# A Fourier block on one core: TensorE's loop unrolled five times, ScalarE's row transfer moved, half of x added on TensorE for three row groups

## The chip, the core and the metric

The kernel runs on one core of a Trainium2 chip. The core has five engines that run at the same time, each with an instruction queue of its own, and wait for each other by semaphores: TensorE (matrix products, PE in the profile, its weight loads PEld), VectorE (DVE), ScalarE (ACT), GpSimd (POOL) and SyncE (SP), which here only issues DMAs. All but GpSimd and SyncE read PSUM, the memory of 8 banks into which TensorE writes. The metric is the device time of one execution in microseconds (us); lower is better.

## The reference

x has the shape (4, 128, 128, 768). For each image and channel: a two-dimensional real Fourier transform, a small two-layer network with complex weights on each block of 96 channels at every frequency, the transform back, and x added.

```python
xf = jnp.fft.rfft2(x, axes=(1, 2), norm='ortho')            # 128 x 65 frequencies
xr, xi = real(xf), imag(xf)      # reshaped to 8 blocks of 96 channels
o1r = relu(xr @ w1[0] - xi @ w1[1] + b1[0])
o1i = relu(xi @ w1[0] + xr @ w1[1] + b1[1])
o2r = o1r @ w2[0] - o1i @ w2[1] + b2[0]
o2i = o1i @ w2[0] + o1r @ w2[1] + b2[1]
o2r, o2i = softshrink(o2r, 0.01), softshrink(o2i, 0.01)
out = jnp.fft.irfft2(o2r + 1j * o2i, s=(128, 128), axes=(1, 2), norm='ortho') + x
```

## The kernel before

The work is cut into 32 units q, one for each image and block of 96 channels. A unit's x stands in SBUF as 128 partitions (one image axis) by 128 rows h by 96 channels; two buffers `xs[0]` and `xs[1]` take turns. Every engine runs its own program: a part ahead, a hardware loop over `STEPS - 1` = 15 steps with two units each (p = 0 and 1), and the last step written out. At the end of a step each engine has a branch back to the loop's first instruction.

Stages of a unit, as TensorE goes through them:

- `keep_warm` (L635): four products whose result nobody reads; `transform_row0` (L499): row 0 of the next unit, which has a way of its own (`row0`, copied by ScalarE in `copy_row0`, L752, and moved by two DMAs that ScalarE issues in `move_row0`, L756 and L757, into row 127 of `ydg` and of `yedge`).
- `inverse_lines` (L515): 26 line groups of 4 or fewer channels, back along h. ScalarE and VectorE copy each result from PSUM to `ydg` and pack the input of the one five groups later into `rings`.
- rows (`first_rows`, `rows`, L646 to L649): 13 row groups g of five rows, back along the other axis. A group has an odd part v and an even part u, in two PSUM banks; the 8 banks hold four groups, so group g waits until VectorE is done with group g - 4 (`uv_ready`). `add_halves` (L972, L979) on VectorE adds half of the folded x to u (into `ucopy`) and to v (into the x buffer) in one instruction of 2 x 480 columns. GpSimd then forms sum and difference of the two (L1051, L1053), which are the output rows, and SyncE stores them in seven batches, followed by the loads of the unit after next.
- `forward_lines` (L493, L494) of the next unit: 26 line groups again. `packer_a` and `mover` say which of ScalarE and VectorE packs the input of a group (L733, L870) and which copies its result (L743, L882). The first five packs stand at the end of ScalarE's previous unit. The line banks are those of the rows, so the first groups wait for the last `uv_ready`.
- mixing (L536 to L629): ten frequency groups, transform along h, first layer in split precision, relu on ScalarE, second layer, shrink on VectorE. The areas that it uses (`zbig`, `zhi`, `hbig`, `biased` and others) lie over `ucopy`. ScalarE's first copy into `zbig` (L768) and VectorE's first shrink therefore wait for the last store batch's rows (`wait_batch`).

TensorE runs the unit boundary as: rows of q, forward lines and mixing of q + 1, then keep-warm of q + 1; its branch stands between the mixing and the keep-warm products. ScalarE's branch stands behind `move_row0`, between rows and forward lines. VectorE's stands between its first mixing operations, GpSimd's behind the last sums.

At the start SyncE issues the transform table, the 16 loads of unit 0 (four pieces of 16 + 16 rows, each in two halves of 64 partitions), the rest of the table, weights, and the 16 loads of unit 1. VectorE folds x (L864, L866: sums and differences of mirrored rows) as the pieces land.

## Time and profile before

| | |
|---|---|
| three runs, us | 4975.51, 4975.89, 4977.45 |
| median, us | 4975.89 |
| profiled execution, us | 4975.77 |
| its span on the core, us | 4973.7 |
| TensorE busy | 4779.5 us, 96% of the span |
| VectorE busy | 4070.3 us, 82% |
| ScalarE busy | 2514.4 us, 51% |
| GpSimd busy | 1028.1 us, 21% |
| DMA over the span | 421.33 MB, mean 85 GB/s |
| mean granted TensorE clock | 0.989 of full speed |

Busy time counts what an engine executes. Matrix products overlap, so a busy TensorE is not one at its best pace. Idle time that "issue" ends is time in which the engine waited for nothing that the profile shows; branches and semaphore instructions are not shown. One fp32 product leaves two records. The profile's times start with the span.

### The profile page before, as it was taken

What the parts mean: (1) busy time and instruction counts of PE and PEld (TensorE: products, weight loads), DVE (VectorE), ACT (ScalarE), POOL (GpSimd) and SP (SyncE); (2) the same over time, 40 slices, a digit from 0 to 9 for tenths busy, and PEclk for the clock granted to TensorE, in tenths of its full rate; (3) what the DMA queues carried; (4) which work ended last, traced back from release to release, by engine and by line L of the source; (5) the groups of instructions that cost most, each with busy time, mean ns of one, the idle gap of its engine ahead of it and who ended that gap; (6) DMA issues with size and microseconds to landing.
All of it is one profiled execution on the core that took longest, in us unless ns stands there. A gap on an engine that the chain in (4) does not pass through costs nothing.

```text
span 4973.7 us, 120408 instructions
## 1 busy us (share of the span) xinstructions
PE 4779.5 (96%) x44930; PEld 3997.2 (80%) x44930; DVE 4070.3 (82%) x6763; ACT 2514.4 (51%) x4290; POOL 1028.1 (21%) x836
## 2 busy tenths in 40 slices
PE   6999999999999999999999999999999999999997
PEld 5888888888888887888878788788888888788886
DVE  5888888888888888888888888788887888888876
ACT  4554455545555445555445554455544555445553
POOL 0220222211222112222022220122211222102222
PEclk9999999999999999999999999999999999999999
DMA  6422544324443234442344423444224453234522
GB/s 110 102 60 51 107 104 104 77 45 95 103 103 87 43 86 103 103 99 44 74 103 103 108 50 62 101 103 108 63 61 88 103 108 78 59 76 103 107 53 51
DMA packets 1079029, 421.33 MB, mean 85 GB/s; under 512 B 1076128, under 2 KB 1076256, under 8 KB 1078432
## 3 DMA queue, kind: packets, MB, share of 16 engines
q1 hardware_dynamic: 1073696, 411.61, 39.1%
q8 instruction: 395, 6.47, 0.6%
q10 hardware_dynamic: 4736, 1.60, 0.1%
q14 instruction: 202, 1.65, 0.1%
HBM read 210.19 MB, written 201.33 MB: 83 GB/s over the span
## 4 chain that ended last, share of the span: by engine, by line
PE 85%; DVE 6%; issue 5%; ACT 3%; POOL 1%; SPq 0%; ACTq 0%; DMA 0%; DVEq 0%; POOLq 0%
PE ps L515 14%; PE ps L611 13%; PE ps L493 10%; PE ps L536 10%; PE ps L620 6%; PE ps L548 5%; PE ps L594 5%; PE ps L582 4%; PE ps L646 3%; PE ps L561 3%; PE ps L569 2%; PE ps L562 2%; ACT rings L733 2%; DVE ydg L954 1%; DVE biased L929 1%
## 5 line engine op out<-in xcount | busy, mean ns | idle before, releaser
L1051 POOL TENSOR_TENSOR whole<-whole 128x480 f32<-128x480 f32 (+1 forms) x416 | 499.4, 1200 | 3904.0 <-DVE whole L979 3904.0
L743 ACT COPY ydg<-ps 128x512 f32<-128x512 f32 (+4 forms) x1024 | 588.3, 578 | 571.4 <-PE ps L494 352.9
L611 PE MATMUL ps<-wts,hbig 128*128 128x192 f32 x4160 | 735.1, 328 | 4.3
L493 PEld LDWEIGHTS ps<-tab,rings 128*64 128x64 f32 x6144 | 675.3, 138 | 78.8 <-ACT rings L733 42.7
L493 PE MATMUL ps<-tab,rings 128*64 128x128 f32 x6144 | 701.2, 275 | 35.1 <-ACT rings L733 34.2
L515 PE MATMUL ps<-tab,rings 128*128 128x128 f32 x6144 | 712.1, 280 | 15.9 <-DVE rings L949 15.9
L515 PEld LDWEIGHTS ps<-tab,rings 128*128 128x128 f32 x6144 | 708.0, 196 | 18.8 <-DVE rings L949 17.9
L494 PE MATMUL ps<-tab,rings 128*63 128x128 f32 x6144 | 701.4, 275 | 0.0
L611 PEld LDWEIGHTS ps<-wts,hbig 128*128 128x128 f32 x4160 | 672.1, 190 | 20.6 <-ACT hbig L791 13.7
L494 PEld LDWEIGHTS ps<-tab,rings 128*63 128x63 f32 x6144 | 675.0, 137 | 0.0
L929 DVE TENSOR_TENSOR biased<-ps,wts 128x768 f32<-128x768 f32 (+1 forms) x544 | 498.9, 917 | 194.0 <-PE ps L620 189.4
L733 ACT COPY rings<-whole 128x508 f32<-128x508 f32 (+1 forms) x608 | 617.5, 1086 | 0.1
L536 PEld LDWEIGHTS ps<-tab,ydg 128*128 128x128 f32 x4032 | 501.3, 191 | 105.5 <-issue 91.6
L536 PE MATMUL ps<-tab,ydg 128*128 128x128 f32 x4032 | 562.3, 282 | 22.0 <-DVE ydg L882 22.0
L768 ACT COPY zbig<-ps 128x512 f32<-128x512 f32 (+1 forms) x544 | 307.6, 569 | 523.2 <-PE ps L536 474.8
L1053 POOL TENSOR_TENSOR whole<-whole 128x480 f32<-128x480 f32 (+1 forms) x416 | 544.6, 1309 | 34.7
L791 ACT ACTIVATE hbig<-ps,wts 128x1024 f32<-128x1024 f32 (+1 forms) x320 | 305.5, 955 | 426.4 <-PE ps L594 426.4
L882 DVE COPY ydg<-ps 127x512 f32<-127x512 f32 (+5 forms) x640 | 388.3, 631 | 157.6 <-PE ps L494 125.8
L954 DVE TENSOR_TENSOR ydg<-biased,clamped 128x768 f32<-128x768 f32 (+1 forms) x512 | 477.7, 933 | 16.7
L907 DVE TENSOR_TENSOR zlo<-zbig,zhi 128x1024 fp32r<-128x1024 f32 (+1 forms) x320 | 326.2, 1019 | 195.4 <-ACT zhi L775 195.4
L875 DVE TENSOR_TENSOR rings<-ydg 128x248 f32<-128x248 f32 (+3 forms) x672 | 379.8, 565 | 114.9 <-PE ps L515 112.2
L782 ACT CAST zsmall_hi<-ps 128x512 fp32r<-128x512 f32 (+1 forms) x320 | 163.2, 510 | 586.2 <-PE ps L548 586.2
(82 smaller groups left out, 8893.8 us busy)
## 6 DMA issues: line engine op xcount, KB each, us to landing
out<-whole SPq DMA_DIRECT2D x704, 240.0 KB, 4.2
whole<-in_x SPq DMA_DIRECT2D x384, 384.0 KB, 6.5
whole<-in_x SPq DMA_DIRECT2D x64, 408.0 KB, 7.8
whole<-in_x SPq DMA_DIRECT2D x64, 360.0 KB, 6.7
out<-whole SPq DMA_DIRECT2D x64, 216.0 KB, 3.5
wts<-in_mix SPq DMA_DIRECT2D x16, 513.0 KB, 4.9
out<-whole SPq DMA_DIRECT2D x64, 120.0 KB, 3.2
out<-whole SPq DMA_DIRECT2D x64, 96.0 KB, 2.9
```

Source lines behind the costliest of these rows:

```text
L493: pe.matmul(o[0:HALF], slot[:, 0:HALF], mat("fwd_w"), start=True, stop=True)
L494: mm = pe.matmul(o[HALF:127], slot[:, HALF:127], mat("fwd_w_odd"), start=True, stop=True)
L515: mm = pe.matmul(ps[:, line_bank(1, g), j * 128:(j + 1) * 128], ring[g % RING][:, j, :], mat("inv_h"), start=True, stop=True)
L536: mm = pe.matmul(ps[:, z_bank(u, h), k * H:(k + 1) * H], t[:, s:s + 2, :].rearrange("p k c -> p (k c)")[:, 0:BIG], mat("fwd_h"), start=Tru ...
L611: mm = pe.matmul(o, hbig[:, k * H:(k + 1) * H], mix_part("w2_big"), start=first, stop=False, skip_group_check=True)
L733: act.copy(*line_pack_moves(p, g)).then_inc(line_packed_act, 1)
L743: act.copy(*line_moves(stage, g)).then_inc(line_act, 1)
L882: dve.tensor_copy(*line_moves(stage, g)).then_inc(line_dve, 1)
L929: dve.tensor_tensor(parts(v), d, b2, ALU.add).then_inc(bias_done, 1)
L954: dve.tensor_tensor(dst, parts(v)[:, :, first:ne, :], parts(c)[:, :, first:ne, :], ALU.subtract).then_inc(shrunk, 1)
L1051: pool.tensor_tensor(xs[p][:, a:b, :], u, xm, ALU.add).then_inc(y_plus, 1)
L1053: pool.tensor_tensor(xm, u, xm, ALU.subtract).then_inc(batch_ready[batch_of(g)], batch_part(g))
```

## The change

Six things are changed.

1. **TensorE's loop** has five steps in its body (`UNROLL`) and runs three rounds in place of 15.
2. **ScalarE**: `move_row0` no longer stands at the end of a unit but inside the forward lines, ahead of line group 6 (`MOVE_ROW0_AT`), and waits for the previous unit's last `uv_ready`. In its place stand three copies (below), and behind them the loop's branch.
3. **Half of x on TensorE**, for row groups 4, 6 and 8 (`ADDED`): the even part gets a third pair of products, half the identity times the folded x rows. ScalarE copies u out of PSUM into `ucopy` and counts `u_copied`; VectorE's operation treats v alone (480 columns, not 2 x 480) and waits for v alone. GpSimd, and TensorE where it takes the bank again (group + 4), wait for `u_copied`.
4. **Waits for the store batches**: ScalarE's first `zbig` copy has none now; its first `zsmall` rounding waits for the batch of group 1, VectorE's first small remainder for that of group 4, ScalarE's first relu for that of group 7. VectorE's first shrink keeps its wait for the last.
5. **Start**: SyncE loads the lower 64 partitions of unit 0 and ScalarE issues the loads of the upper 64, at once.
6. **End**: in the last unit VectorE forms the sums and differences of row groups 6 to 12, after its last `add_halves`; GpSimd does groups 0 to 5.

The first place is the end of ScalarE's loop body and its beginning: end of a unit, branch, forward lines (`rings<-whole` are packs, `ydg<-ps` copies of line results). Before:

```order
L841 ISA
L756 DMA ydg<-row 1x128x96 [waits row0_copied,u_done,v_done]
L757 DMA yedge<-row 1x2x96
L851 REGISTER_ALU
L851 COMPARE_AND_BRANCH
L743 COPY ydg<-ps 127x128x4 [waits line_done]
L733 COPY rings<-whole 128x4x127 [waits line_done]
L743 COPY ydg<-ps 127x128x4 [waits line_done]
L733 COPY rings<-whole 128x4x127 [waits line_done]
L743 COPY ydg<-ps 127x128x4 [waits line_done] x2
```

and changed:

```order
L870 COPY whole<-ps 128x480 [waits u_done]
L881 REGISTER_ALU
L881 COMPARE_AND_BRANCH
L767 COPY ydg<-ps 127x128x4 [waits line_done]
L755 COPY rings<-whole 128x4x127 [waits line_done]
L767 COPY ydg<-ps 127x128x4 [waits line_done]
L755 COPY rings<-whole 128x4x127 [waits line_done]
L767 COPY ydg<-ps 127x128x4 [waits line_done] x2
L755 COPY rings<-whole 128x4x127 [waits line_done] x2
L781 DMA ydg<-row 1x128x96 [waits row0_copied,uv_ready]
L782 DMA yedge<-row 1x2x96
L767 COPY ydg<-ps 127x128x4 [waits line_done]
```

The two DMAs went behind the copies of line groups 0 to 3 and the packs of 5, 6, 8 and 9; the last of the copies of u stands ahead of the branch.

The second place is TensorE in the rows, groups 4 and 5 (`ps<-ydg,tab` are the products of v and u). Before:

```order
L654 ISA
L646 MATMUL ps<-ydg,tab 64x480 [waits uv_ready]
L647 MATMUL ps<-ydg,tab 64x480
L648 MATMUL ps<-ydg,tab 64x480
L649 MATMUL ps<-ydg,tab 64x480
L654 REGISTER_ALU
L646 MATMUL ps<-ydg,tab 64x480 [waits uv_ready]
```

and changed:

```order
L674 ISA
L661 MATMUL ps<-ydg,tab 64x480 [waits uv_ready]
L662 MATMUL ps<-ydg,tab 64x480
L664 MATMUL ps<-ydg,tab 64x480
L665 MATMUL ps<-ydg,tab 64x480
L668 MATMUL ps<-whole,tab 64x480
L669 MATMUL ps<-whole,tab 64x480
L674 REGISTER_ALU
L661 MATMUL ps<-ydg,tab 64x480 [waits uv_ready]
```

The pair `ps<-whole,tab`, which reads the x buffer, was added between group 4's u and group 5's v.

The third place is ScalarE's program from its first instruction, in the changed kernel; before, it began with the table load.

```order
L875 DMA whole<-in_x 64x16x96
L875 DMA whole<-in_x 64x15x96
L875 DMA whole<-in_x 64x16x96 x4
L875 DMA whole<-in_x 64x17x96
L875 DMA whole<-in_x 64x16x96
L755 ACT_TABLE_LOAD [waits pairs_folded]
L755 COPY rings<-whole 128x4x127 [waits cleared]
L755 COPY rings<-whole 128x4x127 x4
L776 COPY row<-ps 128x96 [waits row0_done]
```

Eight of the 16 loads of unit 0 moved here from SyncE, and the row's transfers that followed the last line are gone from this place.

The diff, cut to its core (left out: two semaphores declared, a scratch tile `scrap` in place of `clamped` for the initial settings):

```diff
 NF = HC // HG
+POOL_LAST = 6
+ADDED = (4, 6, 8)
 AREA = 60 * H + 28 * CB
...
 LOAD_AFTER = {2: 0, 4: 1, 6: 2}
+MOVE_ROW0_AT = 6
+UNROLL = 5
 for _name, _n in (("fwd_w", W), ("fwd_w_odd", W), ("fwd_h", H), ("inv_h", H), ("inv_w_even", HALF), ("inv_w_odd", HALF),
-                  ("merge_even", H), ("merge_odd", H)):
+                  ("merge_even", H), ("merge_odd", H), ("half", HALF)):
     COLS[_name] = (_at, _at + _n)
...
     return np.concatenate([fwd_w / 128, fwd_w_odd / 128, fwd_h, inv_h, inv_even / 128, inv_odd / 128,
-                           merge_even, merge_odd], 1).astype(np.float32)
+                           merge_even, merge_odd, np.concatenate([np.eye(64), np.eye(64)]) / 2], 1).astype(np.float32)
...
+        def piece_rows(i):
+            a, e = i * LOAD_ROWS, (i + 1) * LOAD_ROWS
+            return (a, e + (e == HALF)), (H + 1 - e, H + 1 - max(a, 1))
         def odd_rows(g):
             return max(HG * g, 1), min(HG * g + HG, H // 2)
+        def wait_added(engine, q, g):
+            if g in ADDED:
+                engine.wait_ge(u_copied, len(ADDED) * q + ADDED.index(g) + 1)
...
-                def load_piece(n, b, p, i):
+                def load_piece(n, b, p, i, parts=(0, 1)):
                     src = x[bass.ds(b, 1), :, :, bass.ds(n * CB, CB)].rearrange("o h (m t) c -> (o t) m h c", t=2)
-                    a, e = i * LOAD_ROWS, (i + 1) * LOAD_ROWS
-                    for lo, hi in ((a, e + (e == HALF)), (H + 1 - e, H + 1 - max(a, 1))):
-                        for t in range(2):
+                    for lo, hi in piece_rows(i):
+                        for t in parts:
                             sp.dma_start(xs[p][t * HALF:(t + 1) * HALF, lo:hi, :],
...
-                load_x(0, 0, 0)
+                for i in range(PIECES):
+                    load_piece(0, 0, 0, i, (0,))
                 sp.dma_start(tab[:, FWD:TABLE], table[:, FWD:TABLE]).then_inc(table_loaded, 16)
...
-                def quarters(g, cols):
+                def quarters(p, g, cols):
...
                     mv = pe.matmul(v[top], odd[low], yv[low], start=True, stop=True)
-                    pe.matmul(u[top], even[top], yu[top], start=True, stop=True)
-                    mu = pe.matmul(u[low], even[low], yu[low], start=True, stop=True)
+                    alone = g not in ADDED
+                    pe.matmul(u[top], even[top], yu[top], start=True, stop=alone)
+                    mu = pe.matmul(u[low], even[low], yu[low], start=True, stop=alone)
+                    if not alone:
+                        half, xp = mat("half"), xs[p][:, a:b, cols]
+                        pe.matmul(u[top], half[top], xp[top], start=False, stop=True)
+                        mu = pe.matmul(u[low], half[low], xp[low], start=False, stop=True)
                     return mv, mu
-                def rows(q, g):
+                def rows(q, p, g):
                     if g >= 4:
                         pe.wait_ge(uv_ready, NF * q + NF + g - 3)
+                        wait_added(pe, q, g - 4)
                         pe.sem_inc(row_banks_free, 1)
-                    mv, mu = quarters(g, slice(0, CB))
+                    mv, mu = quarters(p, g, slice(0, CB))
                     mv.then_inc(v_done, 1)
-                def first_rows(q):
+                def first_rows(q, p):
                     pe.sem_inc(row_banks_free, 1)
-                    quarters(0, slice(0, c))
+                    quarters(p, 0, slice(0, c))
                     lines_moved(q, 1)
                     pe.sem_inc(row_banks_free, 1)
-                    mv, mu = quarters(0, slice(c, CB))
+                    mv, mu = quarters(p, 0, slice(c, CB))
                     mv.then_inc(v_done, 1)
...
                         inverse_lines(q)
-                        first_rows(q)
+                        first_rows(q, p)
                         for g in range(1, NF):
-                            rows(q, g)
+                            rows(q, p, g)
                         if not (last and p == PAIRS - 1):
...
                 to_inverse(0, 0, 0)
-                with pe.Fori(0, STEPS - 1) as t:
-                    step(t, False)
+                with pe.Fori(0, (STEPS - 1) // UNROLL) as rounds:
+                    for i in range(UNROLL):
+                        step(rounds * UNROLL + i, False)
                 step(STEPS - 1, True)
...
                     for g in range(NG):
+                        if stage == 0 and g == MOVE_ROW0_AT:
+                            move_row0(q)
                         if mover(stage, g) == "act":
...
                 def move_row0(q):
+                    act.wait_ge(uv_ready, NF * q + NF)
                     act.wait_ge(row0_copied, q + 1)
                 def copy_big(q, u, h):
-                    if u == 0 and h == 0:
-                        wait_batch(act, q - 1, NF - 1)
                     act.wait_ge(zbig_done, NP * q + part_at(u, h))
...
                 def round_small(q, u):
+                    if u == 0:
+                        wait_batch(act, q - 1, 1)
                     act.wait_ge(zsmall_done, NU * q + u + 1)
...
                     act.wait_ge(big_mixed, NU * q + u + 1)
-                    if u:
+                    if u == 0:
+                        wait_batch(act, q - 1, 7)
+                    else:
                         act.wait_ge(hbig_read, NU * q + u)
...
                                 pack_lines(q + 1, 1 - p, g)
-                            act.wait_ge(v_done, NF * q + NF)
-                            act.wait_ge(u_done, NF * q + NF)
-                            move_row0(q + 1)
+                        for g in ADDED:
+                            act.wait_ge(u_done, NF * q + g + 1)
+                            act.copy(ucopy[g].rearrange("p h c -> p (h c)"),
+                                     ps[:, row_bank(g), 0:HG * CB]).then_inc(u_copied, 1)
+                first = x[0:1, :, :, 0:CB].rearrange("o h (m t) c -> (o t) m h c", t=2)
+                for i in range(PIECES):
+                    for lo, hi in piece_rows(i):
+                        act.dma_start(xs[0][HALF:W, lo:hi, :], first[1, :, lo:hi, :]).then_inc(x_loaded[0][i], 16)
                 act.wait_ge(cleared, 1)
                 copy_row0(0)
-                move_row0(0)
                 with act.Fori(0, STEPS - 1) as t:
...
                     dve.wait_ge(zsmall_hi_ready, NU * q + u + 1)
+                    if u == 0:
+                        wait_batch(dve, q - 1, 4)
                     dve.tensor_tensor(zsmall_lo[u % 2][0:r, 0:n], ps[0:r, z_bank(u, "small"), 0:n],
...
                     dve.wait_ge(v_done, NF * q + g + 1)
+                    if g in ADDED:
+                        xm, v = xs[p][:, H - b + 1:H - a + 1, :], ps[:, row_bank(g) + 1, 0:HG * CB]
+                        dve.scalar_tensor_tensor(xm, xm, 0.5, v.rearrange("p (h c) -> p h c", c=CB),
+                                                 ALU.mult, ALU.add).then_inc(uv_ready, 1)
+                        return
                     dve.wait_ge(u_done, NF * q + g + 1)
...
+                def last_sums(q, p, g):
+                    a, b = odd_rows(g)
+                    u, xm = ucopy[g][:, 0:b - a, :], mirror(xs[p], a, b)
+                    dve.wait_ge(uv_ready, NF * q + NF + g + 1)
+                    wait_added(dve, q, g)
+                    dve.tensor_tensor(xs[p][:, a:b, :], u, xm, ALU.add).then_inc(last_plus, 1)
+                    dve.wait_ge(last_plus, g - POOL_LAST + 1)
+                    dve.tensor_tensor(xm, u, xm, ALU.subtract).then_inc(batch_ready[batch_of(g)], batch_part(g))
                 def wait_loaded(p, times, i):
...
                             add_halves(q, p, g)
+                        if not fold_next:
+                            for g in range(POOL_LAST, NF):
+                                last_sums(q, p, g)
                         if fold_next:
                 dve.memset(yedge[:], 0.0).then_inc(cleared, 1)
-                dve.memset(clamped[0:1, 0:1], 0.0).then_inc(uv_ready, NF)
-                dve.memset(clamped[0:1, 1:2], 0.0).then_inc(y_plus, NF)
+                dve.memset(scrap[0:1, 0:1], 0.0).then_inc(uv_ready, NF)
+                dve.memset(scrap[0:1, 1:2], 0.0).then_inc(y_plus, NF)
                 for i, ready in enumerate(batch_ready):
-                    dve.memset(clamped[0:1, 2 + i:3 + i], 0.0).then_inc(ready, 2)
+                    dve.memset(scrap[0:1, 2 + i:3 + i], 0.0).then_inc(ready, 2)
                 dve.wait_ge(uv_ready, NF)
...
             def _(pool):
-                def step(t):
+                def step(t, last):
                     for p in range(PAIRS):
                         q = t * PAIRS + p
-                        for g in range(NF):
+                        for g in range(POOL_LAST if last and p == PAIRS - 1 else NF):
                             a, b = odd_rows(g)
                             pool.wait_ge(uv_ready, NF * q + NF + g + 1)
+                            wait_added(pool, q, g)
                             pool.tensor_tensor(xs[p][:, a:b, :], u, xm, ALU.add).then_inc(y_plus, 1)
-                with pool.Fori(0, STEPS) as t:
-                    step(t)
+                with pool.Fori(0, STEPS - 1) as t:
+                    step(t, False)
+                step(STEPS - 1, True)
```

## Rows read from the trace of the kernel before

**Rows 1.** The page, part 4: the chain that ended last, by engine.

```profile
PE 85%; DVE 6%; issue 5%; ACT 3%; POOL 1%; SPq 0%; ACTq 0%; DMA 0%; DVEq 0%; POOLq 0%
```

**Rows 2.** Timeline of TensorE, keep-warm products: start us, us, engine, line, operation, idle before.

```profile
1845.46 1.16 PE L635 MATMUL ps<-tab 128*128 128x128 f32 x8
...
2001.47 2.07 PE L635 MATMUL ps<-tab 128*128 128x128 f32 x8 [2.75 <-issue]
...
2152.81 1.16 PE L635 MATMUL ps<-tab 128*128 128x128 f32 x8
...
4610.31 1.16 PE L635 MATMUL ps<-tab 128*128 128x128 f32 x8
...
4760.24 1.16 PE L635 MATMUL ps<-tab 128*128 128x128 f32 x8
```

**Rows 3.** Waits of TensorE: who waited, for what, us in total, times, longest.

```profile
PE ps L635 <- issue: 39.0, 14, 3.1
```

**Rows 4.** Timeline of ScalarE: start of the run, a step with its branch, one without.

```profile
47.50 0.59 ACT L743 COPY ydg<-ps 127x512 f32<-127x512 f32 x1 [1.98 <-PE ps L494]
...
1886.68 0.59 ACT L743 COPY ydg<-ps 127x512 f32<-127x512 f32 x1 [12.00 <-PE ps L494]
...
4646.31 0.53 ACTq L756 DMA_DIRECT2D ydg<-row  x1
4646.87 0.83 ACTq L757 DMA_DIRECT2D yedge<-row  x1
4647.88 0.59 ACT L743 COPY ydg<-ps 127x512 f32<-127x512 f32 x1 [8.36 <-PE ps L494]
```

**Rows 5.** Timeline of TensorE: first forward product (L493), first mixing products (L536).

```profile
1906.73 1.71 PE L536 MATMUL ps<-tab,ydg 128*128 128x128 f32 x13 [0.67 <-DVE ydg L882]
...
4646.23 0.32 PE L493 MATMUL ps<-tab,rings 128*64 128x128 f32 x1
...
4668.29 1.82 PE L536 MATMUL ps<-tab,ydg 128*128 128x128 f32 x14 [0.69 <-DVE ydg L882]
```

**Rows 6.** Timeline of ScalarE: the five packs at the end of a unit.

```profile
4634.38 5.14 ACT L733 COPY rings<-whole 128x508 f32<-128x508 f32 x5
```

**Rows 7.** Windows: us, busy time of five engines, granted clock, DMA share, GB/s.

```profile
2001.00:2003.00 2.00, 1.53 (x7) 1.53 (x8) 0.00 (x0) 0.00 (x0) 0.00 (x0) 0.50 0.03 8
```

**Rows 8.** Timeline of TensorE: first row products, two groups further on, then forward lines.

```profile
2026.73 0.51 PE L646 MATMUL ps<-ydg,tab 64*64 64x352 f32 x1
...
4634.22 0.51 PE L646 MATMUL ps<-ydg,tab 64*64 64x352 f32 x1
...
4638.21 0.56 PE L646 MATMUL ps<-ydg,tab 64*64 64x480 f32 x1
...
4639.01 0.56 PE L646 MATMUL ps<-ydg,tab 64*64 64x480 f32 x1
...
4647.04 0.27 PE L493 MATMUL ps<-tab,rings 128*64 128x128 f32 x1
...
4647.29 0.32 PE L493 MATMUL ps<-tab,rings 128*64 128x128 f32 x1
```

**Rows 9.** Timeline of VectorE in the rows: twelve operations in one row.

```profile
4635.57 12.65 DVE L979 SCALAR_TENSOR_TENSOR whole<-whole,ps 128x768 f32<-128x768 f32 x12
```

**Rows 10.** Timeline of VectorE at the start: folds behind a landed piece.

```profile
25.69 1.16 DVE L864 TENSOR_TENSOR whole<-whole 128x960 f32<-128x960 f32 x1 [2.56 <-DMA whole<-in_x]
...
33.13 1.16 DVE L864 TENSOR_TENSOR whole<-whole 128x960 f32<-128x960 f32 x1 [5.09 <-DMA whole<-in_x]
```

**Rows 11.** Windows: loads alone; large rows; stores and loads together.

```profile
5.00:10.00 5.00, 0.00 (x0) 0.00 (x0) 0.00 (x0) 0.00 (x0) 0.00 (x0) 1.00 1.30 224
...
33.00:34.00 1.00, 0.00 (x0) 0.00 (x0) 0.87 (x1) 0.00 (x0) 0.00 (x0) 1.00 1.02 378
...
210.00:220.00 10.00, 9.28 (x152) 8.92 (x149) 8.08 (x14) 5.59 (x10) 8.71 (x8) 1.00 1.16 253
```

**Rows 12.** Timeline of SyncE's queue: the stores of the last unit.

```profile
4940.73 30.84 SPq L461 DMA_DIRECT2D out<-whole  x28
```

5 lines of the change are left out of this document (4 added, 1 removed).

## The prediction, written before the changed kernel ran

> **What bounds the kernel now.** I read the chain of waits first. 85% of it is TensorE and 6% VectorE, so what counts is each time that TensorE stands still or runs slowly [rows 1]. One set of 32 (image, channel block) units follows another, and TensorE's four keep-warm products mark the start of each. Near the end of the run one unit takes 4760.24 - 4610.31 = 149.93 us. In the middle a unit with odd number takes 2001.47 - 1845.46 = 156.01, and the even one behind it 2152.81 - 2001.47 = 151.34 [rows 2]. A loop step is an odd and an even unit; the units at the end run where no engine's loop branch is taken any more. So a step costs 307.35 - 2 * 149.93 = 7.5 us more with branches than without. TensorE waited 14 times, 39.0 us in all, for nothing that the profile shows, right before the keep-warm products [rows 3]: 14 of its 15 branches are taken, the last falls through. That is where to look, since the same instructions stand in both kinds of unit.
>
> **ScalarE's branch.** In the odd unit without a taken branch, ScalarE issues the two transfers of row 0 and copies the first group of forward lines at 4647.88, 8.36 us after its last copy. With the branch it does so at 1886.68, after 12.00 us: the stall is 3.64 us [rows 4]. From the keep-warm products to TensorE's first product of the mixing it is then 1906.73 - 1845.46 = 61.27 us against 4668.29 - 4610.31 = 57.98 [rows 5]. The branch costs 3.29 us, in 14 units: 46 us. The change puts the three copies of u where the transfers stood and the branch behind them; the transfers go into the forward lines, before group 6. Is the stall covered there? ScalarE's five packs end at 4634.38 + 5.14 = 4639.5 [rows 6]. The last copied group is 8. By its own pace (below) TensorE ends it 9 * 0.80 + 3 * 0.40 = 8.4 us after the start of the rows at 4634.22, near 4642.6, and the copy ends at 4643.2. With the stall ScalarE is back at 4646.8. TensorE's first forward group, which it has to copy, starts near 4634.22 + 11.6 = 4645.8 and ends 0.9 us later, at 4646.7. So the stall is hidden, narrowly, and I take all **46 us**. Each us that the stall is longer would come straight on 14 units.
>
> **TensorE's branch.** What is left of the 7.5 us: the odd unit has 156.01 - 149.93 - 3.29 = 2.79 us of idleness beyond what the waiting for VectorE would cost anyway, and the even one is 151.34 - 149.93 = 1.41 us longer. The second is the clock: after the idle time the granted clock is 0.50 (1.2 of 2.4 GHz) [rows 7], and the way from keep-warm to the rows takes 2026.73 - 2001.47 = 25.26 us against 4634.22 - 4610.31 = 23.91 [rows 2, 8]. A taken branch costs 4.20 us. The loop of 15 steps becomes 3 rounds of 5: two taken branches instead of 14, 12 * 4.20 = **50 us**. What is late next there is VectorE's last shrink; that wait is in the 149.93 already. The body is five times as long, but the code behind the loop, never run before, is entered by the fall-through without a stall (no idle time before the products at 4760.24 [rows 2]).
>
> **Rows: half of x on TensorE.** Without a wait, TensorE does a row group in 4639.01 - 4638.21 = 0.80 us, two pairs of products of 0.40 each [rows 8]. VectorE does twelve groups in 12.65 us, 1.06 each [rows 9], and there are banks for four groups only, so TensorE ends up at VectorE's pace: 4646.23 - 4634.22 = 12.01 us for 13 groups [rows 5, 8]. The change gives TensorE a third pair in three groups: 13 * 0.80 + 3 * 0.40 = 11.6. VectorE loses half of three operations, 3 * 0.5 us, and is at no point the later one. TensorE becomes the bound and 0.41 us go. The small gap between the first two forward groups (4647.29 - 4647.04, against 0.11 between neighbours [rows 8]) waits for the tenth-last sums and goes with VectorE's gain, 0.14. ScalarE's copies (0.59 us for 512 columns [rows 4]) lie in its idle time; group 8 needs the copy of group 4, done near 4640.1, at 4641.4. 31 units * 0.55 = **17 us**. The pair is not in the trace of before. If it overlapped badly and cost 0.80, the sum would be 12.8 us for the rows, and 20 us lost; if it cost nothing VectorE's pace would bound and some 40 us would be gained. I take 0.40: the same 64x64 shape on the same columns.
>
> **Row 0 inside the lines.** The two issues take 0.53 + 0.83 us [rows 4], at a place where ScalarE has little slack: forward packs run one behind the other and TensorE needs each about 0.7 us after it is done. If the issues stop the engine for their full 1.4 us, TensorE waits about 0.65 in each of 31 units, 20 us; if they pass while earlier copies still run, 0. I take **-3 us**, nearer to nothing, because the five packs stand in one row without a gap [rows 6], so copies are handed over ahead of time. The Trainium skill ("Advanced Engine Details and Errata", Sequencer Loop) says that engine instructions wait in a queue while the sequencer works on others; by that alone this term would be 0.
>
> **Start.** VectorE's folds start when a piece of x has landed, 33.13 - 25.69 = 7.4 us apart [rows 10]; the fold of the last piece leads to TensorE's start. The loads run at 224 GB/s; where stores and loads are mixed it is 253, and with large rows of all partitions once 378 [rows 11]. The change issues the upper half from ScalarE at the same time. Bounds: nothing, or four pieces at 378 (4 * 3.0 = 12 us). At 253, 4 * 7.4 * (1 - 224/253) = 3.4. ScalarE's first line copy no longer stands behind row 0's transfers (idle for 1.98 us before 47.50 [rows 4]): up to 1.7, I take 1.5. Together **5 us**. On the first part the Trainium skill speaks with two voices. "DMA: Bandwidth & Descriptors" (Rules for kernel authors) advises against two transfers to disjoint partition halves, since they share the same 16 engines: 0, and 4862 in all. "SBUF — State Buffer" (Door 1) says that 64 partitions reach only half of the ports, which would make the two halves together up to twice as fast. The 224 GB/s fit the second, but no row has both halves in flight.
>
> **End.** VectorE takes over the last 7 of GpSimd's groups. The stores are 28 issues in 30.84 us [rows 12]; 6.3 MB at 253 GB/s are 24.9. The first three batches keep GpSimd's pace, and VectorE's additions may hold GpSimd up. **1 us**, bounds 0 and 3. The waits for single store batches instead of the last one free ScalarE's first copy of the mixing; TensorE has the other products of that group to do first, so it is worth nothing now, but it lets the earlier arrival through.
>
> **Sum.** 46 + 50 + 17 - 3 + 5 + 1 = 116 us, rounded 117 with the fractions (46.1, 50.4). The profiled execution took 4975.77 (span 4973.7), the median of three runs is 4975.89: no difference here. 4975.8 - 117 = **4859 us**.
>
> **Rivals.**
> 1. The transfers of row 0 do stop ScalarE, or its branch stall isn't covered: up to +20 or so, 4870 to 4885. For it: the slack of 0 to 0.7 us. Chance 0.14.
> 2. The start gains from both halves, and the pair of products is cheap: 4838 to 4849. Chance 0.12.
> 3. The idle time belongs to the change from one step's code to the next, not to the taken branch; unrolling takes nothing away: 4859 + 50 = 4909. Against it: the fall-through without a stall. Chance 0.05.
> 4. The third pair costs twice as much, 0.80: 37 us more, 4896. Chance 0.05.
> 5. Slower: TensorE at group 8 is held by ScalarE's copy of group 4. It has 1.3 us of slack now (4640.1 against 4641.4); beyond that, each us is lost 31 times. It decides the sign from 117/31 + 1.3 = 5.1 us of delay on; with 6 us it would be 4859 + 31 * 4.7 = 5005. Nothing in the rows is that late, since ScalarE is idle there. Chance 0.02.
> 6. The forecast, 4849 to 4870: 0.62.
>
> The forecast with rivals 1 and 2 in part gives the range, 4842 to 4883. Faster by over 0.2% (10 us; about what a measurement of this kernel can tell): 0.96. Within: 0.01. Slower: 0.03.
>
> **What would show it.** Idle time before the keep-warm products twice, not 14 times; units of 149.4 us both in odd and even places; granted clock at full but for two dips; ScalarE's first forward copy 1.0 us after TensorE's first forward product in all units; rows to forward lines in 11.6 us; no wait of TensorE for a pack near group 11; TensorE's start at 34 to 39 us. Wrong would be: waits for u's copies, idle time at each unrolled step, or a forward stage over 22 us.

## The result and the profile after

The changed kernel takes **4894.76 us** (median of 4 runs, 4889.26 to 4895.29), the kernel before beside it 4976.67 us (4975.51 to 4979.08): a ratio of 0.9831, 95% interval [0.9817, 0.9846], 82 us faster. The prediction was 4859 us with a range of 4842 to 4883: the sign was right, the time was outside the range, 36 us too low.

| | before | after |
|---|---|---|
| median | 4976.67 | 4894.76 |
| profiled execution | 4975.77 | 4889.26 |
| its span | 4973.7 | 4887.2 |

The profiled execution of the changed kernel is its fastest one, 5.5 us below the median. Its mean granted clock is 0.998, that of the other three is 0.996, so TensorE ran at the lower clock for less time in it; how much of the 5.5 us that is, isn't shown. All sums below are made against 4889.26.

**Which idle times went.** TensorE's waits, as in [rows 3]: who waited, for what, us in total, times, longest.

```profile
PE ps L530 <- DVE rings L981: 25.6, 30, 0.9
PE ps L551 <- DVE ydg L912: 21.8, 32, 0.8
...
PE ps L650 <- issue: 5.4, 2, 2.8
```

The wait before the keep-warm products (now L650) happens twice, not 14 times. The timeline of TensorE shows the products of a unit without a taken branch, and then the two that stand behind the loop branch where it is still taken:

```profile
1505.29 1.16 PE L650 MATMUL ps<-tab 128*128 128x128 f32 x8
...
1658.80 2.07 PE L650 MATMUL ps<-tab 128*128 128x128 f32 x8 [2.65 <-issue]
...
3169.33 1.15 PE L650 MATMUL ps<-tab 128*128 128x128 f32 x8 [2.75 <-issue]
```

After the first branch the granted clock drops (the products take 2.07 us instead of 1.16), after the second it doesn't here (1.15 us).

**ScalarE's stall is gone from the path.** Timeline of ScalarE, the copy of the last added group, the first forward copy and the idle time before it; above a unit without a branch, below one with it (beside [rows 4]):

```profile
484.16 0.56 ACT L870 COPY whole<-ps 128x480 f32<-128x480 f32 x1 [1.86 <-PE ps L669]
488.41 0.59 ACT L767 COPY ydg<-ps 127x512 f32<-127x512 f32 x1 [3.69 <-PE ps L509]
...
634.94 0.56 ACT L870 COPY whole<-ps 128x480 f32<-128x480 f32 x1 [1.86 <-PE ps L669]
639.18 0.59 ACT L767 COPY ydg<-ps 127x512 f32<-127x512 f32 x1 [3.68 <-PE ps L509]
```

Both wait the same 3.7 us, for TensorE's product. The cover is narrow: the last copy of u ends at 484.72, and with a stall of 3.64 us, as in the kernel before, ScalarE is back at 488.36, 0.05 us ahead of this copy. The first copy starts 1.14 us behind TensorE's first forward product in all 31 units.

**Where the time was lost: the rows.** The first row product, the last even-part product and the first forward product of one unit (timeline of TensorE; beside [rows 5, 8]):

```profile
474.17 0.51 PE L661 MATMUL ps<-ydg,tab 64*64 64x352 f32 x1
...
486.77 0.56 PE L664 MATMUL ps<-ydg,tab 64*64 64x480 f32 x1
487.26 0.32 PE L508 MATMUL ps<-tab,rings 128*64 128x128 f32 x1
```

487.26 - 474.17 = 13.09 us, in every unit; before it was 12.01, and 11.6 were forecast.

The ledger of the profiled executions. Each line is the sum over 31 units of the distance between the first instructions of two stages (the mixing: to its last instruction), read from the timeline:

| us | before | after | difference | the forecast's |
|---|---|---|---|---|
| up to the first keep-warm products | 159.7 | 148.9 | -10.7 | -5 |
| keep-warm and inverse lines up to the rows | 755.7 | 738.6 | -17.1 | -17 (slow clock) |
| rows up to the forward lines | 372.3 | 405.8 | +33.5 | -13 |
| forward lines | 697.7 | 644.8 | -52.9 | -50 (46 + 4) |
| last forward product to the mixing | 33.1 | 32.8 | -0.3 | 0 |
| the mixing | 2844.7 | 2842.8 | -1.9 | 0 |
| its end up to the next keep-warm products | 46.8 | 12.5 | -34.3 | -33 |
| last keep-warm products to the end | 63.7 | 61.1 | -2.6 | -1 |
| row 0's transfers | | | 0 | +3 |

One line has the wrong sign: the rows. Everything else gained what it was to gain, or a little more. The forecast's 17 us for the added pair (13 in the rows, 4 in the forward lines) and its rival 4 (20 us lost, "the third pair costs twice as much") are what the experiments had to tell apart.

### The profile page after: what moved, and what is told of

Read it like the earlier page. It is cut to its first block, busy times and chain, and to the rows that moved or that the text cites. A ratio compares the mean times of both kernels' runs of the same rounds, so it can differ in the third digit from the quotient of the medians.

```text
span 4887.2 us, 121448 instructions
## 1 busy us (share of the span) xinstructions
PE 4766.9 (98%) x45314; PEld 4014.6 (82%) x45314; DVE 4069.1 (83%) x6777; ACT 2569.6 (53%) x4386; POOL 1022.8 (21%) x822
## 4 chain that ended last, share of the span: by engine, by line
PE 89%; DVE 8%; issue 1%; ACT 1%; SPq 0%; DMA 0%; DVEq 0%; ACTq 0%
PE ps L530 14%; PE ps L508 13%; PE ps L626 12%; PE ps L551 10%; PE ps L635 6%; PE ps L563 5%; PE ps L609 5%; PE ps L664 4%; PE ps L597 4%; PE ps L661 3%; PE ps L576 2%; DVE ydg L986 2%; DVE biased L961 2%; PE ps L577 2%; PE ps L584 2%; DVE clamped L963 2%
## 5 line engine op out<-in xcount | busy, mean ns | idle before, releaser
L530 PE MATMUL ps<-tab,rings 128*128 128x128 f32 x6144 | 694.9, 276 | 25.6 <-DVE rings L981 25.6
L530 PEld LDWEIGHTS ps<-tab,rings 128*128 128x128 f32 x6144 | 689.1, 192 | 30.5 <-DVE rings L981 18.2
L508 PE MATMUL ps<-tab,rings 128*64 128x128 f32 x6144 | 679.8, 273 | 1.7 <-ACT rings L755 1.7
L509 PE MATMUL ps<-tab,rings 128*63 128x128 f32 x6144 | 679.8, 273 | 0.0
L551 PE MATMUL ps<-tab,ydg 128*128 128x128 f32 x4032 | 562.2, 282 | 21.8 <-DVE ydg L912 21.8
```

Source lines behind the costliest of these rows:

```text
L508: pe.matmul(o[0:HALF], slot[:, 0:HALF], mat("fwd_w"), start=True, stop=True)
L509: mm = pe.matmul(o[HALF:127], slot[:, HALF:127], mat("fwd_w_odd"), start=True, stop=True)
L530: mm = pe.matmul(ps[:, line_bank(1, g), j * 128:(j + 1) * 128], ring[g % RING][:, j, :], mat("inv_h"), start=True, stop=True)
L551: mm = pe.matmul(ps[:, z_bank(u, h), k * H:(k + 1) * H], t[:, s:s + 2, :].rearrange("p k c -> p (k c)")[:, 0:BIG], mat("fwd_h"), start=Tru ...
```

## Why a pair of products costs 0.80 us: the rows up close

Timeline of TensorE in the kernel before, two groups of rows (start us, us, line; L646 and L647 are the two products of the odd part v, L648 and L649 those of the even part u):

```profile
4638.21 0.56 PE L646 MATMUL ps<-ydg,tab 64*64 64x480 f32 x1
4638.24 0.56 PE L647 MATMUL ps<-ydg,tab 64*64 64x480 f32 x1
4638.36 0.56 PE L648 MATMUL ps<-ydg,tab 64*64 64x480 f32 x1
4638.37 0.56 PE L649 MATMUL ps<-ydg,tab 64*64 64x480 f32 x1
4638.61 0.56 PE L646 MATMUL ps<-ydg,tab 64*64 64x480 f32 x1
...
4638.77 0.56 PE L649 MATMUL ps<-ydg,tab 64*64 64x480 f32 x1
```

All four products start within 0.16 us, and all four come again 0.40 us later. These are not two pairs one behind the other, 0.40 us each, as the prediction read them. Each product has two passes of 0.40 us, and the four run **at the same time**, each on its own quarter of the array: v takes the upper rows to the lower columns and the other way round, u takes upper to upper and lower to lower. A group is 0.80 us because each of its products is.

The added pair in the changed kernel (L668, L669; timeline of TensorE, group 4 and the start of the next):

```profile
477.91 0.56 PE L664 MATMUL ps<-ydg,tab 64*64 64x480 f32 x1
...
478.16 0.56 PE L661 MATMUL ps<-ydg,tab 64*64 64x480 f32 x1
...
478.31 0.56 PE L668 MATMUL ps<-whole,tab 64*64 64x480 f32 x1
...
478.72 0.56 PE L668 MATMUL ps<-whole,tab 64*64 64x480 f32 x1
...
479.12 0.56 PE L664 MATMUL ps<-ydg,tab 64*64 64x480 f32 x1
```

x's upper half has to land on u's upper half, so the pair uses the same two quarters as u. It starts when u's second pass is through (477.91 + 0.40 = 478.31) and the next u starts two passes later. That u goes into another bank, and it comes 0.80 us behind as well: what it waits for is the quarter, not the place where the sum stands. The quarters of u work without a gap from the first group to the last: 0.89 us for the first group, which is divided, 12 + 3 = 15 times 0.804 for the others (two passes of 0.402), and 0.14 up to the first forward product: together 13.09. The next group's v runs beside it and gains nothing.

The Trainium skill says this in "TensorEngine Tiling (Array Packing)", Key Properties: tiles operate independently, and each is tied to its partitions; the table for the 64×64 mode lists the four with their input and output partitions. The rows agree, in both directions: four products at once, and the fifth and sixth have to wait for the tiles of u. The prediction didn't draw on that page.

## The experiments

### How much is one added pair?

**One added group** instead of three.

```diff
-ADDED = (4, 6, 8)
+ADDED = (6,)
```

> The changed kernel with one row group (6) that gets half of x on TensorE, not three (4, 6, 8). Theory Q: the two pairs of a group run at the same time on different quarters of the array, each in two passes of 0.40 us; the added pair needs the quarters of the even part and adds two passes, 0.80 us per added group. In the trace of the changed kernel the even part's quarters do 15 groups of 0.80 and 1.03 us for the divided first group without a gap, 13.09 us. With one added group TensorE needs 13.09 - 1.60 = 11.49, VectorE 12.00 - 0.41 = 11.59: rows to forward lines 11.6 us, 31 * 1.49 = 46 us less than the changed kernel, 4849 us. Rival W: the pair costs 0.40 as forecast, and each added group brings 0.5 us of waiting (for the copy of u or VectorE's order): rows 12.1 us, 31 us less, 4864 us.

Measured: 4855.97 us (4855.47 to 4857.23), ratio 0.9756 [0.9739, 0.9772]. **None at all**, `ADDED = ()`:

> The changed kernel with no added pair at all: rows as before, the other four edits stay. Both theories of the pair expect VectorE's pace in the rows, 12.0 us as before, 31 * 1.09 = 34 us less than the changed kernel: 4861 us. If the three copies of u on ScalarE and the shorter operations on VectorE did any good by themselves, it would be less than 34; if the 13.09 us had nothing to do with the pair, 0. It also gives the sum of the other four edits by itself: 4976 - 4861 = 115 us, where the prediction's terms for them are 46 + 50 - 3 + 5 + 1 = 99 and 4 for the forward lines.

Measured: 4864.16 us (4863.40 to 4864.60), ratio 0.9771 [0.9755, 0.9787]. The other edits gain 114 us by themselves, where the prediction's terms for them give 103. **Two groups**, `ADDED = (5, 8)`:

> The changed kernel with two added groups (5 and 8). By 0.80 us for each on TensorE: rows to forward lines 13.09 - 0.80 = 12.29 us, still set by TensorE and not by VectorE (12.08 - 0.84 = 11.2), so 25 us less than the changed kernel, 4865 to 4870 us, and nothing gained over no added group at all (12.08). If VectorE's relief counted beside TensorE's load, it would lie below 11.6.

Measured: 4872.45 us, one execution. That is 2.5 us above what was expected. One of the two idle times at TensorE's branch is 4.4 us long in it, where the changed kernel has 2.8, and that is 1.7 of them. First row product and first forward product of the third unit in the timeline of TensorE; one added group, then two:

```profile
472.71 0.51 PE L661 MATMUL ps<-ydg,tab 64*64 64x352 f32 x1
...
484.38 0.32 PE L508 MATMUL ps<-tab,rings 128*64 128x128 f32 x1
```

```profile
472.79 0.51 PE L661 MATMUL ps<-ydg,tab 64*64 64x352 f32 x1
...
485.08 0.32 PE L508 MATMUL ps<-tab,rings 128*64 128x128 f32 x1
```

| added groups | rows, even and odd units | set by | time |
|---|---|---|---|
| 0 | 12.16, 12.01 | VectorE | 4864.2 |
| 1 | 11.66, 11.51 | VectorE, TensorE's 11.48 close behind | 4856.0 |
| 2 | 12.29 | TensorE | 4872.5 |
| 3 | 13.09 | TensorE | 4894.8 |

From one to two groups and from two to three the rows grow by 0.7 and 0.80 us: TensorE's price is 0.80. From none to one they shrink by 0.5: there VectorE is the bound, and the shorter operation helps. Theory Q gave 11.6, 12.0 and 12.29; rival W's 12.1 for one group didn't come. The kernel is best with one group, and the three of the change are worse than none: the added pair is worth **+31 us** here (4894.8 - 4864.2), where the prediction had -17. The time with one group is 7 us above the expected 4849. In the traces the rows are 46.6 us shorter than in the changed kernel, but the forward lines are 5.9 us longer and the way from them to the mixing 7.1. The last experiment takes up the second of these.

### Is it the quarter, or any further pair?

**Twice the added work, the second half on the quarters of v.** The odd part then gets half of the wrong half of x, so what it computes is not the transform.

```diff
                         half, xp = mat("half"), xs[p][:, a:b, cols]
+                        pe.matmul(v[low], half[top], xp[top], start=False, stop=True)
+                        mv = pe.matmul(v[top], half[low], xp[low], start=False, stop=True)
                         pe.matmul(u[top], half[top], xp[top], start=False, stop=True)
                         mu = pe.matmul(u[low], half[low], xp[low], start=False, stop=True)
```

> The changed kernel with a second added pair in each of the three groups, on the other two quarters of the array (rows of x's upper half onto the lower partitions of the odd part's bank and the other way round), so that the output is no longer the transform: the odd part gets half of the wrong half of x. Twice the added work for TensorE. Theory Q (time goes by the fuller quarter): the odd part's quarters have room beside the even part's 15 groups, rows 13.1 us and 4895 us as in the changed kernel. Rival S (pairs of products follow one another on the whole array, 0.80 us each): rows 13.09 + 3 * 0.80 = 15.5 us, 4969 us. By the forecast's price of 0.40 for each pair: 14.3 us, 4932 us.

Measured: 4892.95 us (4892.19 to 4894.15), ratio 0.9829 [0.9812, 0.9845]. Timeline of TensorE, the first row product, one product of each added pair of group 4 (L668 on the quarters of v, L670 on those of u), the first forward product:

```profile
474.56 0.51 PE L661 MATMUL ps<-ydg,tab 64*64 64x352 f32 x1
...
478.55 0.56 PE L668 MATMUL ps<-whole,tab 64*64 64x480 f32 x1
...
478.70 0.56 PE L670 MATMUL ps<-whole,tab 64*64 64x480 f32 x1
...
487.65 0.32 PE L508 MATMUL ps<-tab,rings 128*64 128x128 f32 x1
```

The rows take 13.09 us, as with half the added work. The six further products per unit cost nothing, because their quarters had nothing to do. Rival S (4969) and the forecast's price (4932) fall. What counts is the fullest quarter, not the number of products.

### The two branches, one at a time

**TensorE's loop alone**, in the kernel before:

```diff
-                with pe.Fori(0, STEPS - 1) as t:
-                    step(t, False)
+                with pe.Fori(0, (STEPS - 1) // 5) as rounds:
+                    for i in range(5):
+                        step(rounds * 5 + i, False)
```

> The kernel before with one edit: TensorE's loop of 15 steps is 3 rounds of 5 steps. The forecast: 12 taken branches of 4.20 us less, 50 us, 4926 us, with idle time before the keep-warm products twice. Rival (the idle time belongs to the change from one step's code to the next): 14 waits stay, 4976 us. A third case, that ScalarE's branch, still in its old place in this kernel, fills part of the time that TensorE's leaves: between them.

Measured: 4934.55 us (4932.44 to 4936.58), ratio 0.9912 [0.9896, 0.9929]: 43 us, not 50. TensorE's waits and its clock in a unit with ScalarE's stall (windows: us, busy time of five engines, granted clock, DMA share, GB/s), and below it the same stretch in the kernel before:

```profile
PE ps L493 <- ACT rings L734: 33.5, 25, 2.3
...
PE ps L635 <- issue: 6.1, 2, 3.1
...
354.00:357.00 3.00, 3.00 (x36) 3.00 (x34) 0.50 (x2) 3.00 (x5) 2.92 (x3) 0.57 0.87 224
```

```profile
354.00:357.00 3.00, 2.99 (x52) 2.61 (x50) 1.54 (x4) 3.00 (x5) 2.92 (x3) 1.00 0.89 219
```

TensorE's idle time is there twice, as forecast, so rival 3 of the prediction falls. But behind ScalarE's stall, which this kernel still has in each odd unit, the granted clock is now mostly at 1.2 of 2.4 GHz for some 3 us (0.57 in the mean of this window, 1.00 before). The forward lines of the 31 units sum to 706.3 us, not 697.7: 8.6 us come back. Behind ScalarE's branch the granted clock falls to 0.50 in 11 of 14 units here, and did in 3 of 14 in the kernel before. So the two edits aren't independent: with TensorE's own idle time gone, the clock fell behind the other one.

**ScalarE's branch alone**, in the kernel before:

```diff
                     for g in range(NG):
+                        if stage == 0 and g == 6:
+                            move_row0(q)
...
                 def move_row0(q):
+                    act.wait_ge(uv_ready, NF * q + NF)
...
-                            act.wait_ge(v_done, NF * q + NF)
-                            act.wait_ge(u_done, NF * q + NF)
-                            move_row0(q + 1)
...
-                move_row0(0)
```

> The kernel before with one edit: row 0's two transfers go from ScalarE's last place in the step into the forward lines, ahead of group 6, and its branch follows the packs. No copies of u, TensorE's loop as before. The forecast: 46 us less, and 3 us of it lost to the transfers, 4934 us; ScalarE's first forward copy as early in the odd units as in the even ones. If the transfers cost nothing, 31 * 0.45 us more go, since ScalarE's first copy comes 1.14 us behind TensorE's first forward product in the changed kernel and 1.59 in the kernel before, and if TensorE needs that copy: up to 4917 us. Rival (the stall is covered only in part): odd units keep 0.5 to 1 us, 4941 to 4948 us.

Measured: 4924.19 us (4922.17 to 4926.61), ratio 0.9896 [0.9879, 0.9912]: 51 us. Its forward lines sum to 650.3 us, 20.98 in each unit, as in the even units of before: the stall (697.7 - 650.3 = 47.4 us) is wholly covered, and that without the three copies of u. The earlier first copy brings nothing in the units, since 20.98 is what the even ones had before; that is why 4917 wasn't reached. It does so once, at the start, where the first forward copy no longer stands behind row 0's transfers: TensorE's first mixing product starts at 66.03, not 67.73, 1.7 us. These two are 49.1 of the 51 us. The remaining 2 are a balance: behind TensorE's branch the way from the keep-warm products to the rows mostly takes 24.4 us where it mostly took 25.2 to 25.7, which makes 8.9 us in all, and the mixing is 5.8 us longer in all. No run shows why. How little the transfers disturb can be seen in the timeline of ScalarE:

```profile
652.90 1.10 ACT L745 COPY ydg<-ps 127x512 f32<-127x512 f32 x2
653.75 0.53 ACTq L759 DMA_DIRECT2D ydg<-row  x1
653.86 1.16 ACT L733 COPY rings<-whole 128x508 f32<-128x508 f32 x1
654.31 0.63 ACTq L760 DMA_DIRECT2D yedge<-row  x1
```

The two issues (0.53 and 0.63 us) run while the engine does its copies and packs, one behind the other. This is what the Trainium skill says ("Advanced Engine Details and Errata", Sequencer Loop), and what the prediction had named as a term of 0 and not taken.

### The start: two halves, or two queues?

**All first loads from SyncE**, as before the change (the loop of issues on ScalarE is left out).

> The changed kernel with all of the first loads issued by SyncE, as before. The folds should stand 7.2 to 7.4 us apart again, not 4.8, TensorE's first product move from 30.4 to about 39.2 us, and the span be 8.8 us longer, 4896 us. If the earlier start were due to something else (the waits around it), it would stay at 30.4.

Measured: 4900.47 us, span 4898.5, one execution. VectorE's folds behind a landed piece (timeline), first in the changed kernel, then here; beside [rows 10]:

```profile
14.77 1.16 DVE L894 TENSOR_TENSOR whole<-whole 128x960 f32<-128x960 f32 x1 [2.64 <-DMA whole<-in_x]
...
24.35 1.16 DVE L894 TENSOR_TENSOR whole<-whole 128x960 f32<-128x960 f32 x1 [2.42 <-DMA whole<-in_x]
```

```profile
18.34 1.16 DVE L890 TENSOR_TENSOR whole<-whole 128x960 f32<-128x960 f32 x1 [5.00 <-DMA whole<-in_x]
...
32.85 1.16 DVE L890 TENSOR_TENSOR whole<-whole 128x960 f32<-128x960 f32 x1 [5.00 <-DMA whole<-in_x]
```

Two pieces take 9.58 us in the changed kernel and 14.51 here. TensorE's first forward product goes from 32.86 to 41.37: 8.5 us are the loads.

**Both queues, but each writes the lower 64 partitions first, then the upper, piece by piece:** SyncE the low image rows, ScalarE the mirrored ones.

> The changed kernel with the first loads on both queues, but divided by rows of the image: SyncE takes the low rows, ScalarE the mirrored ones, and each first those of the lower 64 partitions and then those of the upper, so that at any time both queues write to the same half of the partitions. If the gain of the start comes from writing both halves at once, the folds stand 7.2 to 7.4 us apart, TensorE starts at about 39 us. If it comes from a second queue, 4.8 us apart and 30.4 us. Both queues drift apart somewhat, so a value between them is possible: up to 6 us apart, TensorE at 35 us.

**The same, with all lower halves ahead of all upper ones:**

```diff
-                for i in range(PIECES):
-                    lo, hi = piece_rows(i)[0]
-                    for t in range(2):
+                for t in range(2):
+                    for i in range(PIECES):
+                        lo, hi = piece_rows(i)[0]
```

> The changed kernel with the first loads on both queues (SyncE the low rows of the image, ScalarE the mirrored ones), and all those of the lower 64 partitions ahead of all those of the upper. In the kernel with the loads divided by rows the rate jumped between about 219 GB/s (that of one queue) and 325 GB/s (that of the changed kernel). Theory H (what counts is whether both halves of the partitions are written at the same time): 219 to 225 GB/s for nearly the whole load, with 325 only where one queue is a half ahead; the loads of 6.3 MB end at about 2.5 + 28.7 = 31 us, the first fold is late, near 18 us. Rival (a second queue is enough, and the jumps are something else): 290 to 325 GB/s throughout, loads done near 22 us.

Measured: 4896.14 and 4901.60 us, one execution each. The GB/s that the DMA engines moved in the first 32 us, in 40 slices of 0.8 us; first the changed kernel, then all from SyncE, then piece by piece, then the strict order:

```profile
GB/s 0 0 143 206 225 288 217 279 272 311 326 325 324 326 325 324 326 323 325 326 324 323 327 325 324 326 324 325 287 257 420 392 266 209 225 216 207 233 212 238
```

```profile
GB/s 0 0 159 53 173 257 260 215 218 221 218 227 221 225 208 229 212 228 214 226 215 219 223 209 229 210 234 209 225 217 221 222 212 232 215 228 216 223 224 235
```

```profile
GB/s 0 0 140 225 255 253 218 278 244 219 300 325 279 260 325 306 219 317 325 243 276 324 290 226 326 323 231 287 328 295 219 239 278 425 362 274 210 221 219 223
```

```profile
GB/s 0 0 153 181 250 250 216 211 211 207 209 206 197 191 196 205 207 199 202 204 211 272 324 274 215 209 211 202 210 212 207 209 206 210 210 209 204 203 214 235
```

There are two levels, 219 and 325. One queue gives 219, and two queues that write to the same half give no more (about 205). Two queues that write to different halves give 325. Where the pieces alternate, the queues drift, and the rate jumps between the two levels as they meet and part: folds 5.4 us apart, TensorE's first forward product at 35.3. In the strict order the rate reaches 324 only around 17.6 us, where one queue is in the upper half and the other still in the lower. A second queue alone is worth nothing; both halves at once are worth 1.5 times the rate. One queue stays at 219 although its transfers go to the two halves in turn; that it works on them one behind the other would explain it, but no run shows that. The first fold came at 23.27, not at 18: it waits for rows of the upper partitions, which come after all of the lower ones (3.15 MB, 15.4 us at 205 GB/s), and the expectation had put that too short.

Of the two pages of the Trainium skill that the prediction set against each other, the trace sides with "SBUF — State Buffer" (Door 1), which makes bandwidth depend on the ports that the partitions reach. "DMA: Bandwidth & Descriptors" (Rules for kernel authors) advises against two transfers to disjoint halves because they serialize. Here they don't: 7.26 us per piece from one queue (14.51 / 2), 4.79 with the halves side by side.

### The end

**GpSimd does all last sums**, `POOL_LAST = NF`.

> The changed kernel with GpSimd doing all thirteen groups of the last sums again, as before. From the last unit's keep-warm products to the end of the span: 61.1 us in the changed kernel, 63.7 in the kernel before. If VectorE's share of the last sums is what shortened it, 63.7 here, 2.6 us more; if something else in the end did (a faster ScalarE, the copies of u), 61.1 stays.

Measured: 4895.40 us, span 4893.3, one execution; from the last keep-warm products to the end of the span 4893.3 - 4829.7 = 63.6 us. SyncE's queue, the stores of the last unit, in the changed kernel and here (beside [rows 12]):

```profile
4856.85 28.25 SPq L476 DMA_DIRECT2D out<-whole  x28
```

```profile
4860.41 30.71 SPq L476 DMA_DIRECT2D out<-whole  x28
```

VectorE's share of the last sums is worth 2.5 us, the whole gain of the end.

### Without any taken branch, and VectorE's tail

**One added group, and TensorE's steps written out:**

```diff
-                with pe.Fori(0, (STEPS - 1) // UNROLL) as rounds:
-                    for i in range(UNROLL):
-                        step(rounds * UNROLL + i, False)
-                step(STEPS - 1, True)
+                for t in range(STEPS):
+                    step(t, t == STEPS - 1)
```

> The kernel with one added group (the first experiment), and TensorE's 15 loop steps and the last one written out, so that TensorE takes no loop branch at all. The two that are left cost 152.69 - 149.49 = 3.20 and 0.60 behind it, and 2.74 and 0.63: 7.2 us, so 4856.0 - 7.2 = 4848.8 us, no idle time before any keep-warm products and the granted clock at full up to the last unit. Rival: the longer run of code without a jump makes TensorE wait for its instructions somewhere else; then the 7 us come back, 4856 us.

Measured: 4851.96 us (4850.22 to 4853.08), ratio 0.9750 [0.9734, 0.9767]. 4 us of the expected 7.2 came. The idle time before the keep-warm products (5.9 us in two times) is gone, the granted clock is at full up to the last unit, and nothing as long appeared anywhere else: for no reason that the profile shows TensorE waited twice in the forward lines, 1.2 and 0.3 us. The Trainium skill ("Runtime: NRT & Kernel Launch", Instruction fetch mechanics) says that code streams in by itself as long as it runs straight on, and that a taken branch to code that isn't at hand stalls. The kernel behaves so: straight code of 16 steps has no idle time above those 1.2 us, a taken branch has 2.6 to 3.2 us (once 4.4). That fetching the code is what takes this time, no run shows. What took part of the gain back is in TensorE's waits (the first line is the kernel with one added group and the loop, the second the one written out):

```profile
PE ps L551 <- DVE ydg L912: 28.9, 32, 1.1
```

```profile
PE ps L551 <- DVE ydg L910: 35.0, 32, 1.3
```

TensorE waits 6.1 us longer for VectorE's last copy of the forward lines. So the last experiment takes work from VectorE just there.

```diff
-    return "act" if g < RING + 2 or g % 3 != 1 else "dve"
+    return "act" if g < RING + 2 or g % 3 != 1 or g >= 22 else "dve"
```

> The kernel with one added group and TensorE's loop written out (4852.0 us), with VectorE's last two packs of the forward lines (groups 22 and 25) given to ScalarE. There TensorE waits 35.0 us in 32 times for VectorE's last copy of a forward group, up to 1.3 us, before the mixing. If VectorE is what bounds the end of the forward lines, up to 0.3 us go from each of 31 units, the wait falls below 27 us and the time to about 4843 us. Rival: ScalarE's packs come too late for TensorE or its own copies, and the wait only changes its name: 4850 to 4860 us.

Measured: **4840.70 us** (4840.31 to 4841.04), ratio 0.9728 [0.9711, 0.9744]. That is the fastest kernel of this study, 54 us below the changed one.

```profile
PE ps L551 <- DVE ydg L910: 25.3, 32, 0.8
```

The wait fell by 9.7 us, the time by 11.3. Once TensorE no longer was the bound in the rows, VectorE was the bound at the end of the forward lines: this wait is 21.8 us in the changed kernel, 28.9 with one added group.

## Why the prediction was wrong, point by point

- **The reading of the rows, the step that failed.** "0.80 us, two pairs of products of 0.40 each [rows 8]". The 0.80 was right, the division was not. The prediction quoted only the first product of each group (L646), and from one product per group nothing can be seen of how the four lie in time. From this the price of the third pair, "I take 0.40: the same 64x64 shape on the same columns", was half of what it is. It is 0.80, because the pair queues behind u on the same two quarters, so the rows take 13.09 instead of 11.6, 31 * 1.49 = 46 us. The same rows of the kernel before, all four lines of a group, would have shown it.
- **Rival 4 was the case that happened**, with its mechanism (20 us lost in the rows) and nearly its time, 4896 against 4894.8. It had a chance of 0.05 and lay outside the range, though the bound of 0.80 was in the text. The divided first group and the step to the forward lines (1.03 us where 0.80 was put) make the rows 13.09, not 12.8. That the time came out so close is luck: these 9 us more are made up for by the start and the other terms that gained more than forecast.
- **ScalarE's branch, 46 us.** 47.3 in the trace (52.9 in the forward lines less 31 * 0.18 for the small gap), 47.4 with the edit alone. The cover held, in the changed kernel by some 0.05 us if the stall is 3.64; the forecast had put ScalarE's last copy of u 9 us behind the start of the rows, and it ends 10.55 behind it.
- **TensorE's branch, 50 us.** 34.3 idle and 17.1 of clock and line stages, 51.4 in all. Alone in the kernel before it gave 43: the price is right only with ScalarE's stall gone too, which the prediction didn't say.
- **The small gap in the forward lines, 4 us.** 20.98 became 20.80 per unit, 5.6 us. With one or no added group it stays at 20.98: it goes with VectorE's lead in the rows, as said, but TensorE pays for that lead.
- **Row 0's transfers, -3 us.** 0. The lower bound was right.
- **The start, 5 us.** 10.7: 8.5 from the loads, 1.7 from the first copy and the rest from differences between executions. The size of the first part was missed. The upper bound of 12 held; the chosen 3.4 came from a stage in which stores and loads are mixed, and that stage says nothing on two halves.
- **The end, 1 us.** 2.6, from VectorE's sums alone.
- Two of the signs that were to show the forecast came out otherwise: units of 150.6 and 150.8 us instead of 149.4, from the rows, and TensorE's first product at 30.4 us, not at 34 to 39, from the loads.
- The errors don't cancel: +46 in the rows, and some 16 us the other way in all the other terms, 30 in the profiled execution. The rest of the 36 is that this execution lies 5.5 us below the median.
- Not settled: why the other executions of the changed kernel are 5 to 6 us above the profiled one. In the profiles of its five variants with the same rows, both taken branches are followed by slow clock, and the time between the start and the last unit is 2 to 5 us longer; in this profile only the first is, and briefly. No run separates this from other causes.

## What to carry to other kernels

Before a product is priced, look at all products of its neighbourhood in the timeline and at the quarter of the array that each uses: small products are free on a quarter that is idle and cost their whole time on one that is full. Moving work from the engine that is the bound to the next one pays only up to the point where both are level, here one group of 13; compute both engines' totals for each number of moved groups, and take the crossing. A step that is worth something only while another stall exists, or only without it, has to be costed together with that stall.

## What the runs showed of the hardware that I had not expected

- Four 64x64 products run at once: 13.09 us for the rows with 6 or with 12 added products per unit, as long as the 6 further ones use the idle quarters.
- Loads to one half of the partitions run at 205 to 219 GB/s from one queue or from two; to both halves at once at 325.
- After TensorE's idle time of 2.6 to 3.2 us at a taken branch the granted clock is 0.50 for a few us in most places and not in others (the second branch of the changed kernel). With the idle time at TensorE's branch gone, it fell behind ScalarE's stall more often (0.57 in a window where it had been 1.00; in 11 of 14 units where it had been in 3), 8.6 us in all.
